# A graph network's two layers on one core: sort steps in chosen slots, hidden-layer products split, slices made ahead, transfers of 128 rows

## What is computed

```python
edge_index = jnp.stack([src, dst])
xn = _layernorm(x, axis=-1)
x = x + _L0_gnn_ref(xn, edge_index, ...) + _L0_mix_ref(xn[None], ...)[0]
x = x + _L0_ffn_ref(_layernorm(x, axis=-1)[None], ...)[0]
xn = _layernorm(x, axis=-1)
x = x + _L1_gnn_ref(xn, edge_index, edge_type_8, ...) + _L1_mix_ref(xn[None], ...)[0]
x = x + _L1_ffn_ref(_layernorm(x, axis=-1)[None], ...)[0]
```

```python
msg = _layernorm(msg.reshape(N, L, C) @ Wm, g1, b1)
h = jnp.concatenate([x, msg], axis=-1) @ W1
h = jax.nn.relu(h) @ W2
return x + _layernorm(h, g2, b2)
```

## Time and profile before

| | us |
|---|---|
| median of 3 runs (7690.67 to 7696.88) | 7695.04 |
| the profiled execution | 7685.26 |
| its span | 7683.4 |
| TensorE busy | 5374.4 (70%) |
| VectorE busy | 5151.8 (67%) |
| ScalarE busy | 1872.6 (24%) |
| GpSimd busy | 3468.0 (45%) |

### The profile page before, as it was taken

How to read it: one execution, slowest core, us unless ns; L and a number is a source line. 1 busy time by engine, 2 the same in 40 slices (tenths; PEclk the granted TensorE clock), 3 DMA queues, 4 the chain that set the end, 5 groups by cost and what they waited for, 6 DMA issues and landing times. The chain is left out here.

```text
span 7683.4 us, 87333 instructions
## 1 busy us (share of the span) xinstructions
PE 5374.4 (70%) x25164; PEld 3713.1 (48%) x25164; DVE 5151.8 (67%) x11681; ACT 1872.6 (24%) x4564; POOL 3468.0 (45%) x3441
## 2 busy tenths in 40 slices
PE   5877774555555655534789978997999999951991
PEld 2446663333333443422464434444777777841661
DVE  6457777888888877775447677777676767760332
ACT  0233333222222332312314400010222222210220
POOL 0000003777777777740000076666776767715006
PEclk8998886777777777767989989999999999965995
DMA  4100003445455555540003332232333333332223
GB/s 140 50 29 1 1 1 80 123 125 125 124 125 126 135 132 129 131 88 20 0 25 129 133 98 84 82 87 83 95 99 94 99 93 99 98 66 85 63 63 109
DMA packets 310191, 665.92 MB, mean 87 GB/s; under 512 B 77974, under 2 KB 173964, under 8 KB 302717
## 3 DMA queue, kind: packets, MB, share of 16 engines
q0 software_dynamic: 180352, 455.22, 23.7%
q1 hardware_dynamic: 129383, 205.31, 7.8%
HBM read 546.52 MB, written 113.55 MB: 86 GB/s over the span
## 5 line engine op out<-in xcount | busy, mean ns | idle before, releaser
L2054 POOL DMA_INDIRECT ag_rows<-table,row_src x1612 | 1591.0, 987 | 1747.0 <-POOLq L2849 1022.9
L1142 POOL DMA_INDIRECT at_rows<-table,row_dst x1612 | 1634.4, 1014 | 491.0 <-issue 448.9
L1308 PE MATMUL at_p_a<-at_rows,at_hot 128*125 128x264 f32 x3224 | 1139.4, 512 | 998.0 <-issue 987.3
L1308 PEld LDWEIGHTS at_p_a<-at_rows,at_hot 128*125 128x125 f32 x3224 | 710.1, 246 | 1185.4 <-issue 1045.9
L1271 DVE TENSOR_TENSOR acc<-acc,at_p_a 125x264 f32 x1612 | 687.3, 426 | 244.4 <-PE at_p_a L1308 101.5
L2164 DVE TENSOR_TENSOR mo_prod<-mo_far,mo_twice 125x256 f32<-125x256 f32 x1600 | 580.2, 419 | 51.5 <-issue 45.0
L2424 PE MATMUL mo_p_e<-ag_rows,ag_hot 128*125 128x256 f32 x1612 | 465.2, 413 | 150.3 <-DVE acc L2263 84.7
L1094 POOL PARTITION_ALL_REDUCE sb_top<-sb_top x1 | 0.4, 397 | 1221.4 <-DVE sb_top L1065 1221.4
L1258 DVE TENSOR_TENSOR at_rows<-at_rows 128x1024 f32<-128x1024 f32 x496 | 496.7, 1022 | 21.8 <-ACT at_rows L1190 21.1
L2263 DVE TENSOR_TENSOR acc<-acc,mo_p_e 125x256 f32 x806 | 336.8, 418 | 249.3 <-PE mo_p_e L2424 100.5
L2424 PE MATMUL mo_p_m<-ag_rows,ag_hot 128*125 128x256 f32 x1612 | 461.4, 410 | 42.0 <-DVE acc L2263 41.3
(11 more groups left out here) (490 smaller groups left out, 9776.7 us busy)
## 6 DMA issues: line engine op xcount, KB each, us to landing
at_wide<-node_t SPq DMA_DIRECT2D x124, 406.2 KB
table<-rt_row SPq DMA_DIRECT2D x50, 1000.0 KB
at_rows<-table,row_dst POOLq DMA_INDIRECT x1612
ag_rows<-table,row_src POOLq DMA_INDIRECT x1612, 2.8
moe_in<-ones SPq DMA_DIRECT2D x1, 13440.0 KB
ex_space<-moe_in SPq DMA_DIRECT2D x105, 128.0 KB, 2.2
moe_out<-ex_space SPq DMA_DIRECT2D x105, 128.0 KB, 1.7
table<-row SPq DMA_DIRECT2D x50, 128.9 KB
```

The lines of the kernel that those rows point to most:

```text
L1142: pool.indirect_dma_start(out=rows[n % 3][:, g, :], out_offset=None, in_=m.table0, in_offset=bass.IndirectOffsetOnAxis(ap=row_i[:, n * G + ...
L1308: pe.matmul(p_a[k % BANKS][0:P, 0:TW], hot[n % 2][:, g, :], rows[n % 3][:, g, :], start=True, stop=True).then_inc(s_agg, 1)
L2054: pool.indirect_dma_start(out=rows[:, i % RING, j, :], out_offset=None, in_=m.table1, in_offset=bass.IndirectOffsetOnAxis(ap=row_i[:, 2 * ...
```

## The change

Four edits, in three blocks.

1. `early_plan` keeps the plan of the first part. In the second part a sort step stands after the slots with slot % 10 in (4, 5, 6, 7, 9) until all are placed.
2. On TensorE in the second part of the first stage, the products of a hidden quarter with the two input chunks (`hidden(i, o, 0)`) stand apart from those with the message chunks (`hidden(i, o, 2)`): for quarters 2 and 3 in slot 2, for 0 and 1 in slot 4 ahead of the transposes, behind a wait for the older pair's output in `p_b` (`s_hn`). TensorE waits once for all weights (`s_w1`) before the pairs.
3. `slice_weights`: three buffers of rows, `norm` and `copy_xt` apart on ScalarE, with the exponential of tile n first, `turn` and `logits` apart on TensorE, and all tiles written out instead of looped.
4. `experts`: both indirect transfers take 128 partitions. For this VectorE clears the partitions 96 to 127 of the row tiles in five instructions at the start of the block (ScalarE waits for each), GpSimd writes places of 300 spare rows into the last three partitions of `place`, the two tables grow by 3 x 128 rows, and the spare rows of `moe_out` are filled behind `moe_in` in the first stage.

The diff, cut: the renaming of buffers, declarations and lines that only follow are left out.

```diff
+SORT_SLOTS = (4, 5, 6, 7, 9)
...
-    plan = ["sort"] * (2 * COUNTED) + ["rows", "rows", "sort"] * SORTED
-    return plan + ["rows"] * max(0, 6 + 2 * NT + 2 + LEAD + SPAN * PAIRS + TAIL + 1 - 2 * SORTED)
+    first_rows = 6 + 2 * NT + 2
+    plan = ["sort"] * (2 * COUNTED) + ["rows", "rows", "sort"] * (first_rows // 2)
+    left = SORTED - first_rows // 2
+    for slot in range(-LEAD, SPAN * PAIRS + TAIL):
+        plan.append("rows")
+        if slot % SPAN in SORT_SLOTS and left > 0:
+            plan.append("sort")
+            left -= 1
+    return plan + ["sort"] * left + ["rows"]
...
+                    sp.dma_start(m.moe_out[MC * LANES:, :].rearrange("(p a) (h c) -> p (a h) c", p=LANES, h=2),
+                                 m.ones[:, :].unsqueeze(1).broadcast_to((128, 6, 128))).then_inc(s_fill, 16)
...
+                    pe.wait_ge(s_w1, 128)
                     pe.wait_ge(s_blocks, 1)
+                    def hidden(i, o, from_c):
+                        at = 2 * P * (o % 2)
+                        for c in (from_c, from_c + 1):
+                            moving = xnt[:, c, 2 * P * i:2 * P * i + 2 * P] if c < 2 else zt[:, c - 2, :]
+                            mm = pe.matmul((p_b, p_kv)[o // 2][:, at:at + 2 * P], w1[:, c, 128 * o:128 * o + 128], moving,
+                                           start=c == 0 and o % 2 == 0, stop=c == 3, skip_group_check=True)
+                        return mm
...
+                        i = pair_at(slot, 2)
+                        if i is not None:
+                            for o in (2, 3):
+                                hidden(i, o, 0)
                         i = pair_at(slot, 4)
                         if i is not None:
+                            if i >= 1:
+                                pe.wait_ge(s_hn, i)
+                            for o in (0, 1):
+                                hidden(i, o, 0)
                             pe.wait_ge(s_xm, i + 1)
                             for c in range(2):
                                 for j in range(2):
@@ -937,14 +964,7 @@
                             i = pair_at(slot, 5 + o)
                             if i is not None:
                                 pe.wait_ge(s_zt, i + 1)
-                                if o == 0 and i >= 1:
-                                    pe.wait_ge(s_hn, i)
-                                p_h = (p_b, p_kv)[o // 2]
-                                at = 2 * P * (o % 2)
-                                for c in range(4):
-                                    moving = xnt[:, c, 2 * P * i:2 * P * i + 2 * P] if c < 2 else zt[:, c - 2, :]
-                                    mm = pe.matmul(p_h[:, at:at + 2 * P], w1[:, c, 128 * o:128 * o + 128], moving,
-                                                   start=c == 0, stop=c == 3)
+                                mm = hidden(i, o, 2)
...
+                def norm(n):
+                    if n >= 3:
+                        act.wait_ge(s_sum, n - 2)
+                    act.activation(xn[n % 3][:, 0:C], m.x[:, n, :], ACT.Identity, scale=m.rstd[:, n:n + 1],
+                                   bias=m.nmr[:, n:n + 1]).then_inc(s_xn, 1)
+
+                def copy_xt(n):
                     act.wait_ge(s_tr, n + 1)
+                    if n >= 2:
+                        act.wait_ge(s_log, n - 1)
+                    act.copy(xt[n % 2][:, :, :].rearrange("p c n -> p (c n)"), p_t[:, 0:2 * P]).then_inc(s_xt, 1)
+
+                norm(0)
+                copy_xt(0)
+                norm(1)
+                copy_xt(1)
+                for n in range(NT):
                     act.wait_ge(s_sub, n + 1)
+                    act.activation(w[n % 2][:, :], w[n % 2][:, :], ACT.Exp).then_inc(s_exp, 1)
+                    if n + 2 < NT:
+                        norm(n + 2)
                     act.wait_ge(s_wt, n + 1)
+                    act.copy(swt[:, n, :, :].rearrange("p o n -> p (o n)"), p_w[:, 0:4 * P]).then_inc(s_swt, 1)
+                    if n + 2 < NT:
+                        copy_xt(n + 2)
...
+                def turn(n):
                     pe.wait_ge(s_xn, n + 1)
-                    if not first(n):
+                    if n >= 1:
                         pe.wait_ge(s_xt, n)
                     for c in range(2):
-                        mm = pe.transpose(p_t[:, P * c:P * c + P], xn[u][:, 128 * c:128 * c + 128], m.ident[0:P, 0:P])
+                        mm = pe.transpose(p_t[:, P * c:P * c + P], xn[n % 3][:, 128 * c:128 * c + 128], m.ident[0:P, 0:P])
                     mm.then_inc(s_tr, 1)
+
+                def logits(n):
                     pe.wait_ge(s_xt, n + 1)
-                    if later(n):
+                    if n >= 2:
                         pe.wait_ge(s_sub, n - 1)
                     for c in range(2):
-                        pe.matmul(p_l[u][0:P, :], xt[u][:, c, :], w_log[:, c, :], start=c == 0, stop=False)
-                    pe.matmul(p_l[u][0:P, :], m.ones3[:, 0:P], b_log[:, :], start=False, stop=True).then_inc(s_log, 1)
-
-                front(0, 0)
-
-                def step(n, u, last):
-                    if not last:
-                        front(n + 1, 1 - u)
+                        pe.matmul(p_l[n % 2][0:P, :], xt[n % 2][:, c, :], w_log[:, c, :], start=c == 0, stop=False)
+                    pe.matmul(p_l[n % 2][0:P, :], m.ones3[:, 0:P], b_log[:, :], start=False, stop=True).then_inc(s_log, 1)
+
+                turn(0)
+                turn(1)
+                logits(0)
+                for n in range(NT):
+                    if n + 1 < NT:
+                        logits(n + 1)
                     pe.wait_ge(s_sw, n + 1)
-                    if not first(n):
+                    if n >= 1:
                         pe.wait_ge(s_swt, n)
                     for o in range(4):
-                        mm = pe.transpose(p_w[:, P * o:P * o + P], w[u][:, 128 * o:128 * o + 128], m.ident[0:P, 0:P])
+                        mm = pe.transpose(p_w[:, P * o:P * o + P], w[n % 2][:, 128 * o:128 * o + 128], m.ident[0:P, 0:P])
                     mm.then_inc(s_wt, 1)
+                    if n + 2 < NT:
+                        turn(n + 2)
                     for o in range(4):
-                        mm = pe.matmul(p_s[o][:, 0:C + 1], w[u][:, 128 * o:128 * o + 128], xn[u][:, :],
+                        mm = pe.matmul(p_s[o][:, 0:C + 1], w[n % 2][:, 128 * o:128 * o + 128], xn[n % 3][:, :],
                                        start=False, stop=False, skip_group_check=True)
                     mm.then_inc(s_sum, 1)
...
+                        if n % GT == 0:
+                            act.wait_ge(s_clear, n // GT + 1)
...
+                pool.iota(place[:, :, :], [[3 * NT, 2], [3, NT]], base=MC * LANES - P, channel_multiplier=1).then_inc(s_tri, 1)
                 pool.wait_ge(s_xn, pairs)
                 pool.wait_ge(s_place, 1)
                 for n in range(NT):
                     for k in range(2):
                         pool.indirect_dma_start(out=m.moe_in, out_offset=bass.IndirectOffsetOnAxis(ap=place[:, k, n:n + 1], axis=0),
-                                                in_=xn[:, n, :], in_offset=None).then_inc(s_scat, 16)
...
-                dve.wait_ge(s_tri, 2)
+                for g in range(NT // GT):
+                    dve.memset(space[96:128, GT * g:GT * g + GT, :], 0.0).then_inc(s_clear, 1)
+                dve.wait_ge(s_tri, 3)
...
-        m.moe_in = nc.dram_tensor("moe_in", (MC * LANES, C), F32).ap()
-        m.moe_out = nc.dram_tensor("moe_out", (MC * LANES, C), F32).ap()
+        m.moe_in = nc.dram_tensor("moe_in", ((MC + 3) * LANES, C), F32).ap()
+        m.moe_out = nc.dram_tensor("moe_out", ((MC + 3) * LANES, C), F32).ap()
```

More of the change, by code:

```diff
@@ L377, in _ @@
                 sp.wait_ge(s_kept, 16)
-                sp.wait_ge(s_fill, 32)
+                sp.wait_ge(s_fill, 48)
             @block.vector
@@ L1472, in slice_weights @@
         sb, ps, sem = m.scope(nc, ctx)
-        xn = [sb(f"sl_xn{u}", [P, C + 1], F32) for u in range(2)]
+        xn = [sb(f"sl_xn{u}", [P, C + 1], F32) for u in range(3)]
         xt = [sb(f"sl_xt{u}", [128, 2, P], F32) for u in range(2)]
@@ L1488, in _ @@
                 act.wait_ge(s_zero, 1)
-                def front(n, u):
-                    if later(n):
-                        act.wait_ge(s_sum, n - 1)
-                    act.activation(xn[u][:, 0:C], m.x[:, n, :], ACT.Identity, scale=m.rstd[:, bass.ds(n, 1)],
-                                   bias=m.nmr[:, bass.ds(n, 1)]).then_inc(s_xn, 1)
-                    act.wait_ge(s_tr, n + 1)
-                    act.copy(xt[u][:, :, :].rearrange("p c n -> p (c n)"), p_t[:, 0:2 * P]).then_inc(s_xt, 1)
-                front(0, 0)
-                def step(n, u, last):
-                    if not last:
-                        front(n + 1, 1 - u)
+                def norm(n):
[4 more added lines that the diff above has]
+                def copy_xt(n):
```

(28 more changed lines are left out.)

9 lines of the change are left out of this document (5 added, 4 removed).

## The result

| | before | changed | |
|---|---|---|---|
| median of the runs, us | 7692.9 (7690.1 to 7696.9) | 7519.9 (7517.3 to 7525.1) | ratio 0.9776 [0.9759, 0.9793] |
| profiled execution, us | 7685.3 | 7525.1 | span 7683.4, 7523.4 |

The change saves 173 us; 141 were forecast. The profiled executions differ by 160.0, and the table follows these 160 through the stages: each row compares the start of the same instruction in both traces.

The account below looks back on a forecast made before the run. Bounds: a loop through VectorE and TensorE in the first stage, TensorE waiting in every slice tile, GpSimd's issue in the experts' transfers. 38 + 63 + 47 - 6 - 1 = 141 off the 7695.0 median gives 7554 us; range 7490 to 7608.

Parts of the forecast that it names:

- first stage: Mixing pairs: moved products and sort steps take the mean pair from 27.43 to 25.9 us, saving 38 us in 25 pairs.
- slices: Slice stage: TensorE's waits of 1.32 us a tile go, leaving 5.1 with TensorE the bound; 63 us saved, ends 30 and 75.
- transfers: Experts: scatters and gathers of 128 rows instead of 125 issue faster on GpSimd, 100 of each; 47 us saved.
- clears: Start of the experts: five clears on VectorE, 10.7 us in all, less 4.4 of idle time; 6 us lost.
- fill: First stage: 0.39 MB more to fill lengthens the issue of the row store behind it on SP; 1 us lost.
- The clock's part: First stage: the clock falls in TensorE's pause and costs 2.5 us in 15 of 25 pairs, 26.9 against 24.4.
- VectorE's wait of 6.1 us goes: First stage: query product done 9.9 us after the message's statistics start, so VectorE reaches the query minimum unhindered at 13.93.
- (a): First stage rival: the pause costs no clock or is filled in every pair; 24.4 us a pair, 7516 us, chance 0.25.
- (b): First stage rival: no gain, the chain of exponential, half and two products at low clock fills 27.4; 7592 us, chance 0.12.
- (c): Experts rival: 128 rows do not shorten the issue of the transfers; 7601 us, chance 0.08.
- (d): Slice stage rival: only half the gain, VectorE or ScalarE taking over as the bound; 7586 us, chance 0.05.
- (e): First stage rival: the clock never rises, 33.4 us a pair; 7742 us, slower by 47, chance 0.02.

Follow-up runs that it names:

- e2_products: The kernel before with only the four first-half products moved ahead of the wait for the message, sort steps left in place: 8072.7 us, ratio 0.9877.
- e8_unrolled: The kernel before with only the slice stage's two-tile loop written out for all 50 tiles on three engines: 8275.5 us in one run, beside 8276.4.
- e7_filler_short: The changed kernel with 8 filler matmuls a pair on TensorE behind the last half product: 8070.6 us in one run, beside 8276 for the kernel before.
- e6_query_first: The changed kernel with sort steps put back, query product ahead of all second halves, clears on GpSimd behind the constant places: 8012.7 us, ratio 0.9677.
- e9_places_late: e6_query_first with GpSimd's clears ahead of the constant places, and VectorE waiting for the places only where it writes over them: 7397.6 us, ratio 0.9623.

## Why the prediction was right, and where it wasn't

**The total**: 141 forecast, 173 measured, inside the range. The parts, forecast and measured: first stage 38 and 34.8; slices 63 and 90.1; transfers 47 and 52.0; clears -6 and -7.9; fill -1 and about 0. They add up to 141 and 169. The 6.4 us at the program's start stand in no part of the forecast, and 3.9 of them went to the sort step ahead of the first pair. The 32 that the total lies over the forecast are mainly the 27 of the slices.

**First stage.** The mechanism held: VectorE's wait goes, a pause of 5 us opens before the output product, and the clock falls in it. 25.9 us a pair were forecast, 25.98 came. Three things inside are less good. The pairs with turn steps were taken as the quick ones, 24.4; the pairs measured lie between 23.4 and 29.6 us, and turns among them wait for VectorE (a wait of 2.39 us ahead of one at 1056.33, and the granted clock is 0.50 in 1057 to 1059, in such a pair). The clock's part was sized with a fall 2.5 us behind the last matmul and 7.7 us a pair at the low level; in the pair shown the last matmul ends at 1028.46 and the clock falls in 1032 to 1033 (0.66), and a mean of 0.90 makes it (1 - 0.90) x 2 x 25.98 = 5.2 us a pair. So the mean is right by some luck, and its make-up isn't. And the step "so VectorE's wait of 6.1 us goes, and its own row of work sets the pair up to 13.93" had the query product done at 9.9: 4 us in which VectorE did sort steps that nothing asked for at that point. The rows for pricing the two edits apart were there, and priced apart they give 22.1 us a pair without the moved steps (expected for e2_products; 22.90 came). The forecast took the edit as one.

**Slices.** Wrong by 27 us, above its upper end of 75. The step that failed is "without them a tile is 5.1": labelled waits were taken off, but groups of matmuls that follow each other without a wait overlap by 0.1 to 0.2 us, at three places of the tile, 0.5 in all. Writing out the loop is not it: that gave 0.19, inside the labelled wait (e8_unrolled). That TensorE bounds the new tile held: VectorE waits 0.7 twice a tile and TensorE not at all.

**Transfers.** 28.0 + 24.0 = 52.0, the upper end. A scatter took 960 instead of 1178 and the step from one to the next went from 1.558 to 1.275 us, more than the issue itself; 47 had taken 1.6 off for no row's sake.

**Clears.** 10.7 us was sized as five durations of 2.15; with the 0.48 between them they take from 6699.69 to 6712.57, 12.9, and less the 4.4 of idle time that is 8.5, about the 7.9 measured. "The constant places on GpSimd fall in an idle stretch" was wrong as it stood: they come 9.89 us behind the operation before them and VectorE waits for them, and only the clears hid it. In return GpSimd's first constants came 6.4 us sooner at the program's start.

**Fill.** The second fill stands 49.97 us in issue on SP, but the row store behind it took 1.02 instead of 20.73, and the lead of 6.4 us at the program's start is 7.5 at the last row store. Its -1 was right within what can be seen.

**Rivals.** (a) falls with e7_filler_short: the pause does cost clock, 1.2 us a pair. (b) falls with the 34.8 us; (c) with 960 and 946 ns; (d) with the 4.60 us a tile, which went the other way; (e) had the clock near 0.5, and it was 0.90.

## What to carry to other kernels

Price each half of an edit by itself, even where they are made together: here one half was worth 4.5 us a pair, and the other, worth 1.5 by itself, took 3.1 of that away again. Put an engine's independent work where it hands over and waits to get back, not where it already has work in order; and when waits go between groups of matmuls, count that the groups close up as well. Give an indirect transfer a row count with a large divisor up to 16, and before moving an added constant or clear, look what it was hiding.

## What the hardware showed that was not expected

- The issue time of an indirect transfer goes with the largest divisor of its row count up to 16: 942 ns for 112 rows, 1319 for 124.
- GpSimd's operation for the constant places starts 9.89 us behind the one ahead of it (10.58 in e6_query_first, 7.59 behind the clears in e9_places_late). In every kernel that has it, the first operation of this kind at the program's start stands 0.30 to 0.31 us behind the one before it, and 6.75 to 7.45 in every kernel that hasn't: as if one late start had moved from the program's start to the experts. What the engine does meanwhile, and how one execution could reach into the next, no row shows; it stays open.
- The kernel before took 6 to 8% longer on two other chips (8176 us on one, 8276 and, at another time, 8180 on the other). In the traces nearly all of it lies in the two stages of gathers (2449.8 against 2124.2 us, 2571.5 against 2314.2), with the issue of a gather nearly the same, 946 to 949 ns. The cause wasn't looked for.
- The best kernel tried is e9_places_late: products ahead, sort steps where they were, the query product first, slices and 128-row transfers as changed, clears and places off VectorE's path: 7397.6 us, 0.9623 [0.9609, 0.9637] of the kernel before.
